# Quantised levels transposed by SyncE's transfers instead of by TensorE and ScalarE, in 29 of 32 units

## The reference

```python
def layer(x):
    a = layernorm(x)
    Q, K, V = heads(a @ Wq.T + bq), heads(a @ Wk.T + bk), heads(a @ Wv.T + bv)    # 16 heads of 32
    s = Q @ K.T / sqrt(32) - (i - j)              # causal: -inf where j > i
    x = x + layernorm(merge(softmax(s) @ V) @ Wo.T + bo)
    h = layernorm(x) @ hadamard(512)
    scale = max(|h|, axis=-1) / 7
    q = clip(round(h / scale), -8, 7) * scale     # 4-bit levels, one scale a token
    w = ternary(weight) * mean(|weight|, axis=1)
    return x + layernorm(q @ w.T)
```

## Time and profile before

| | |
|---|---|
| median of 3 runs | 1180.91 us (1174.84 to 1181.16) |
| the profiled execution | 1179.27 us, of which 1177.6 us lie between its first and last instruction (the span) |
| TensorE (PE) busy | 1095.7 us, 93% |
| VectorE (DVE) busy | 986.9 us, 84% |
| ScalarE (ACT) busy | 707.6 us, 60% |
| GpSimd (POOL) busy | 591.3 us, 50% |
| granted TensorE clock, mean | 0.97 |
| transfers issued by SyncE (hardware queue) | 141.34 MB, 57.9% of the time of 16 DMA engines |

### The profile page before, as it was taken

One profiled execution on the slowest core, in us unless ns is written; L12 is line 12 of the kernel. 1 busy time (PEld: TensorE's weight loads), 2 busy tenths in 40 slices (PEclk: granted clock), 3 DMA queues, 4 the chain that ended last, 5 costly groups with the idle time before them and its releaser, 6 DMA issues.

```text
span 1177.6 us, 44905 instructions
## 1 busy us (share of the span) xinstructions
PE 1095.7 (93%) x18656; PEld 733.6 (62%) x18656; DVE 986.9 (84%) x2558; ACT 707.6 (60%) x1494; POOL 591.3 (50%) x719
## 2 busy tenths in 40 slices
PE   4898999999999999999999999999999999998551
PEld 3565666666666666666666666666666676765220
DVE  5748998889988888899888888899888889987572
ACT  5444666666666666666666666656666666565431
POOL 1333465555545655555545555555555555554322
PEclk9989999999999999999999999999999999999775
DMA  9647667666667776666677775557677766554230
GB/s 275 151 80 143 133 159 163 144 138 142 124 128 150 159 163 153 133 136 135 128 145 155 164 159 135 132 127 138 143 149 164 156 149 132 124 115 108 57 72 37
DMA packets 204687, 161.81 MB, mean 137 GB/s; under 512 B 150432, under 2 KB 150688, under 8 KB 204384
## 3 DMA queue, kind: packets, MB, share of 16 engines
q1 hardware_dynamic: 199600, 141.34, 57.9%
q0 software_dynamic: 4880, 17.57, 4.2%
HBM read 40.87 MB, written 16.78 MB: 49 GB/s over the span
## 4 chain that ended last, share of the span: by engine, by line
PE 69%; DVE 21%; issue 3%; DMA 2%; SPq 2%; ACT 1%; POOL 1%; POOLq 0%; DVEq 0%; ACTq 0%
PE f_job L1286 45%; PE f_st L1387 5%; PE f_o L1404 5%; PE f_o L1409 4%; PE f_job L1449 3%; DVE f_bst L986 2%; PE f_job L1362 2%; DVE f_stage L940 2%; DVE f_rmax L954 2%; PE f_job L1431 2%; DVE f_inverse L978 1%; PE f_job L1439 1%; DVE f_x L1010 1%; DVE f_o L976 1%; DVE f_x2l L1040 1%
## 5 line engine op out<-in xcount | busy, mean ns | idle before, releaser
L471 POOL TENSOR_SCALAR_AFFINE_SELECT f_PT<-f_PT 64x512 f32<-64x512 f32 (+1 forms) x256 | 203.3, 812 | 159.1 <-ACT f_PT L638 108.1
L486 POOL TENSOR_TENSOR f_square<-f_stage 128x512 bf16<-128x512 f16 x128 | 130.9, 1045 | 92.1 <-ACT f_stage L616 79.2
L477 POOL TENSOR_TENSOR f_OTl<-f_o,f_OTh 128x256 f16<-128x256 f32 x128 | 85.0, 671 | 143.8 <-ACT f_OTh L656 143.8
L1286 PE MATMUL f_job<-f_xTh,f_wqh 128*128 128x256 f16 x512 | 140.8, 275 | 14.5 <-DVE f_wkl L815 14.4
L616 ACT ACTIVATE f_stage<-f_job,f_bias 128x256 f16<-128x256 f32 x256 | 106.4, 467 | 76.5 <-PE f_job L1286 69.2
L1286 PE MATMUL f_job<-f_xTl,f_wqh 128*128 128x256 f16 x512 | 140.2, 274 | 0.0
L1286 PE MATMUL f_job<-f_xTh,f_wql 128*128 128x256 f16 x512 | 140.1, 274 | 0.0
L1286 PE MATMUL f_job<-f_xTh,f_wkh 128*128 128x256 f16 x512 | 140.0, 274 | 0.0
L1286 PE MATMUL f_job<-f_xTh,f_wkl 128*128 128x256 f16 x512 | 140.0, 273 | 0.0
L1286 PE MATMUL f_job<-f_xTl,f_wkh 128*128 128x256 f16 x512 | 140.0, 273 | 0.0
L940 DVE SCALAR_TENSOR_TENSOR f_stage<-f_job,f_bias,f_stage 128x256 f16<-128x256 f32 x256 | 111.0, 476 | 32.7 <-ACT f_stage L616 32.7
(11 more groups left out here) (181 smaller groups left out, 2928.6 us busy)
## 6 DMA issues: line engine op xcount, KB each, us to landing
f_stacks<-f_stage SPq DMA_DIRECT2D x380, 128.0 KB
f_xin<-x SPq DMA_DIRECT2D x32, 512.0 KB, 6.4
f_x<-x SPq DMA_DIRECT2D x32, 512.0 KB, 4.7
out<-f_z POOLq DMA_DIRECT2D x32, 512.0 KB, 3.5
f_Vmix<-f_V SPq DMA_DIRECT2D x32, 256.0 KB, 6.2
f_Vmix<-f_V SPq DMA_DIRECT2D x64, 128.0 KB, 6.4
f_stacks<-rows_const SPq DMA_DIRECT2D x3, 512.0 KB, 4.9
f_stacks<-wqT SPq DMA_DIRECT2D x2, 512.0 KB, 5.8
```

The lines of the kernel that those rows point to most:

```text
L471: nc.gpsimd.affine_select(out=d, in_=d, compare_op=ALU.is_ge, fill=0.0, base=odd * SUB, pattern=[[0, 4], [0, TP], [1, SUB]], channel_multi ...
L477: nc.gpsimd.tensor_tensor(OT[s % 2][1][:, g, :], o32[:, g % 2, :], OT[s % 2][0][:, g, :], ALU.subtract).then_inc(OTl_made, 1)
L486: nc.gpsimd.tensor_tensor(square[:, 2 * m + pair, :], h, h, ALU.mult).then_inc(squared, 1)
L1286: mm = pe.matmul(dst, lhs[a](c), rhs[b](c), start=(n == 0), stop=(n == 3 * KC - 1))
```

## The change

For units 0 to 28 (`by_queue` = 29) the levels are transposed by one transposing transfer for each tile in SyncE's queue, `turn_levels`, from `q16` straight into `qT`. `turn_q` and `keep_q` go from the loops of TensorE and ScalarE; they stay for units 29, 30 and 31, whose calls stand behind the loops. `turn_levels(k - 1, 0)` is placed behind `restack(n, 0)` and `turn_levels(k - 1, 1)` behind `restack(n, 2)`, ahead of `turn_x(m)`. `second` waits for the transfer's semaphore, and so does `x2_high`, which writes over `q16`'s memory. Nothing else of the arithmetic or of the order changes.

```diff
+        q_moved = [sem(f"q_moved{t}") for t in range(TP)]
...
+        by_queue = STEPS - 3
+
+        def levels_read(k, t):
+
+            return (q_moved[t], 16 * (k + 1)) if k < by_queue else (q_turned, TP * (k - by_queue) + t + 1)
+
...
+            def turn_levels(k, t):
+
+                sp.wait_ge(q_made, TP * k + t + 1)
+                until(sp, f_product, TP * (k - 1) + t + 1)
+                sp.dma_start(qT[:, t], q16[:, t, :], transpose=True).then_inc(q_moved[t], 16)
...
                 restack(n, 0)
+                if has(k - 1):
+                    turn_levels(k - 1, 0)
                 restack(n, 1)
                 restack(n, 2)
+                if has(k - 1):
+                    turn_levels(k - 1, 1)
                 if has(m):
                     turn_x(m)
...
             def x2_high(k, t):
                 act.wait_ge(folded, 2 * (TP * k + t) + 2)
-                until(act, q_turned, TP * (k - 1) + t + 1)
+                if k:
+                    act.wait_ge(*levels_read(k - 1, t))
...
             def keep_q(k, t):
-                act.wait_ge(q_turned, TP * k + t + 1)
+                act.wait_ge(*levels_read(k, t))
...
                     round_levels(k - 1, 1)
-                    keep_q(k - 1, 0)
...
                 invert(s, 0)
-                if has(k - 1):
-                    keep_q(k - 1, 1)
                 invert(s, 1)
...
-                       "q": lambda k, t: (qT_made, TP * k + t + 1), "f": lambda k, t: (z_made, TP * k + t + 1)}
+                       "q": lambda k, t: (qT_made, TP * (k - by_queue) + t + 1), "f": lambda k, t: (z_made, TP * k + t + 1)}
...
                     pe.wait_ge(tern_kept, KC)
-                pe.wait_ge(qT_made, TP * k + t + 1)
+                if k < by_queue:
+                    pe.wait_ge(q_moved[t], 16 * (k + 1))
+                else:
+                    pe.wait_ge(qT_made, TP * (k - by_queue) + t + 1)
...
                     out_product(k, 0)
-                if has(k - 1):
-                    turn_q(k - 1, 0)
                 keys(s, 1, 0)
...
                 if has(k - 1):
-                    turn_q(k - 1, 1)
                     second(k - 1, 0)
```

## The result

The changed kernel takes 1228.76 us (median of 4 runs, 1227.11 to 1235.84) against 1179.60 for the kernel before beside it: ratio 1.0431, 95% interval 1.0412 to 1.045. It is slower, as forecast, but by 49 us where 21 were forecast, and outside the range. The profiled execution has a span of 1228.4 us, 50.8 more than before.

A forecast was written before the change was run, and what follows sets the result against it. TensorE, busy for 93% of the span, was taken as the bound. Per unit -0.46 for removed transposes and +1.2 of wait give +0.74, over 29 units +21.5 on 1179.27: forecast 1200 us, range 1176 to 1219.

The forecast's parts named there:

- T1's wait: TensorE at `second(k,1)` waits for tile 1's transposing transfer, issued behind the twelfth restack transfer: 1.2 us a unit.
- the evictions' going can hurt nothing: ScalarE loses two evictions a unit, 35 us in all; TensorE does not stand for ScalarE, so counted as nothing.
- VectorE could not become the bound: Over a whole unit, VectorE's 29.64 us fit in 33.17 less 0.46, so it was no case with a gain.
- The removal, -13.3: Two groups of four TensorE transposes go from each of 29 units: 0.46 us a unit, 13.3 us, all on the path.
- Hidden: Rival: tile 1's transfer lands before TensorE comes to `second(k,1)`; 1175.8 us, or 1166 with no wait; 12%.
- T0, nothing: Tile 0's transfer, behind the fourth restack transfer, has over 5 us before `second(k,0)` needs it: no wait.
- The 0.35: Taken off the 1.55 us wait at `second(k,1)`: VectorE catches up during the stall, so the next restack starts sooner.
- The landing: In a full queue tile 1's transfer lands when `turn_x`'s first transfer landed before; mean wait at `second(k,1)` 1.55 us.
- The untrimmed 1.55: Mean wait in us a unit at `second(k,1)` with full DMA engines, before 0.35 is taken off for VectorE's catching up.
- Worse: Rival: tile 1's transfer pays its queueing and tile 0's issue in full, 2.35 less 0.35 us; 1224 us; 8%.
- What is moved behind T0 and T1, nothing: Eight restack transfers, `turn_x`, `turn_x2` and `x2_high` come later in or after SyncE's queue, but cost TensorE no wait.
- Signs looked for: TensorE standing before `second(k,1)`, 58 transfers, second landing 3 to 4 us after issue, unit 15 at 33.9, ScalarE down 35 us.

The follow-up runs named there:

- the order mended: Kernel with the transfers left out, plus a wait: GpSimd masks group 2 only after VectorE has folded tile 0; 1174.55 us, ratio 0.9965.
- The hold on GpSimd: GpSimd's masking of group 2 waits until VectorE has folded tile 0; added to the changed kernel with the late load: 1194.37 us, ratio 1.0136.
- the late load: Changed kernel with `load_front` (512 KB) issued behind `turn_x`, not ahead of the restack transfers; 1201.0 us, ratio 1.0202.
- T0 alone: Changed kernel with only tile 0's levels sent by SyncE's queue, tile 1's staying with TensorE and ScalarE; 1177.78 us, ratio 0.9991.
- T1 ahead: Changed kernel with tile 1's transfer moved ahead of the last four restack transfers; 1202.79 us, ratio 1.0214.

## Why the prediction was wrong

The step that failed is the price of T1's wait: 1.2 us a unit in the sum, 1.85 in the trace, 19 of the missing 28 us. Some 8 more are the granted clock, which the sum had at nothing. The direction, the place of the wait and its releaser were right. A second step, that the evictions' going can hurt nothing, failed as well, but it is hardly in the measured time: the runs without the transfers show it.

**What bounds the kernel.** Right for TensorE. That VectorE could not become the bound was wrong: VectorE was within a microsecond of it in one stretch of each unit.

**The removal, -13.3.** TensorE does lose this work. But the two evictions were taken as nothing, and their going could "hurt nothing". This does not hold: together with the transposes their removal costs 14 us instead of giving 13 (1192.81 with the transfers left out), since the eviction of tile 1 had held GpSimd's masking behind VectorE's foldings. Reordering that one eviction in the kernel before costs 21 us (1201.72). Even with the order mended the removal gives 4 to 5 us, not 13.3 (1174.55): the waits for `qk_low` rise from 3.1 to 7.0, those before `scores(n,3)` by 2.2, and 0.9 more stand before `second(k,1)`. The sentence on VectorE as a bound summed a whole unit (29.64 in 33.17 us); within one stretch, `y_out(k,1)` to `scale_out(k-1,0)`, it had 0.6 us. In the changed kernel itself little of this shows, since TensorE's wait for T1 comes first and VectorE catches up in it: the rows show its longer foldings, not a wait for them. The hold on GpSimd was not tried on that kernel as it is; with the late load, where T1's wait is 31.6 us, it is worth 6.6. All of it would have shown had T1 come in time: then, as in the rival *Hidden*, the kernel would have stood near 1193 and not at 1166 to 1176. That rival was out of reach for a reason that I hadn't read.

**T0, nothing.** Its own landing is waited for in only 4 units (2.8 us). Its cost is in what it moves back, and there the sum was right for T1: T1's issue at `turn_x`'s old place plus 1.26 is 17.42 us after the unit's start, and 17.42 is what the 29 units show.

**T1's wait, 1.2 us a unit.** It measured 1.85 in the mean, 53.6 us for 34.8: 19 of the missing 28 us. TensorE's arrival was right (19.29 us after the unit's start, 19.70 less 0.46 forecast). Two terms failed. The 0.35 taken off for VectorE's catching up: the restack did start sooner, 7.00 for 7.45 in the mean, but SyncE then needed 10.32 us from its start to its end, where 8.56 before and 1.26 for T0 make 9.82, so the 0.45 gained was spent in the queue. That is 10 us. The landing: T1 lands 3.59 us behind its issue in the mean and TensorE goes on 3.73 behind it, at 21.14, where `turn_x`'s landings in the four units of the earlier trace rows had given 20.83, another 9 us. The untrimmed 1.55 gives 1211, the landing 1220 and the clock 1228, beside 1228.76 measured; the waits for T0 (+2.8) and the shorter ones for `qk_low` (-1.4) come on top. The case *Worse*, at 8%, named 1224 with a wait of 2.0 us, nearer to the 1.85 than my 1.2. Beside `turn_x`'s landing of before, TensorE goes on 0.3 later; *Worse* had 0.45 later (0.8 less 0.35), my sum 0.35 earlier.

**The clock, not in the sum.** 8.1 us. It is missing from the forecast because the earlier trace rows show 1.00 and TensorE waits for nothing in that unit. The forecast itself had such waits in it; its mean of 1.2 us hid a spread that the earlier trace rows already showed (from 0 to 2.4 us in four units), and it is the upper end of the spread that pays twice.

**What is moved behind T0 and T1, nothing.** Half right. In the kernel after TensorE has indeed waited longer at `second(k,1)` than the restack needs. But the cover is T1's own wait: where that goes, the same transfers are waited for (some 7 us with T0 alone, 25 with T1 ahead).

**Signs looked for.** The wait before `second(k,1)` and T1's landing at 3 to 4 us came as described. ScalarE's busy time fell by 21.5, not 35, and VectorE rose by 20, which the list did not have and which was the sign to follow.

## What to carry to other kernels

Before work is taken from an engine with time to spare, ask whom it had been holding back: here 0.6 us of ScalarE's kept GpSimd behind VectorE on their shared access to SBUF, and one `wait` on GpSimd is worth 18 us where that order is lost. Judge the slack of the second engine stretch by stretch between its hand-overs, not by its share of a unit. A transfer put into a full queue costs its own wait and that of whatever it moves back; where single waits come near 2 us and more, some 1.35 us of half clock sometimes come on top; so sum over the spread of the waits and not over their mean.

## What the runs showed of the hardware

- VectorE's operations with two SBUF inputs and GpSimd's masking stand for one another: behind a masking 0.15 us becomes 0.67 and 0.42 becomes 0.88 to 0.92. The other way round GpSimd stood for VectorE's whole row of six foldings: two maskings took 2.71 for 1.28 us.
- The granted clock fell to 0.50 in the middle of a kernel 11 times over four kernels, each time behind a wait of 1.84 us or more of TensorE, and never in the kernels whose waits were all shorter. Waits of up to 2.7 us also passed without a fall.
- A transposing transfer of 128 KB takes 1.25 us of SyncE's queue to issue, against 0.67 for a restack transfer of 128 KB in the mean (0.60 in the median), and lands 2.4 us after its issue with little beside it and 3.5 in this queue (up to 5.8). Taking a 512 KB load out of the way brought the median from 3.5 to 2.5.
